# Three of layer 2's eight contraction tiles as sums of fp32r products of halves

## The reference, cut to what matters

```
x = x + x @ W.T + 0.5 * (x @ A[label]) @ Bw.T        # layer 0: one weight, low rank 32
x = x + quantise(x)                                  # layer 1: 8 thresholds, levels 0 to 63
x = x + x @ weight[adapter].T                        # layer 2: a 1024 x 1024 weight per adapter
x = x + (x @ B3[adapter].T) @ A3[adapter].T          # layer 3: low rank 16
```

## Time and profile before

| | us |
|---|---|
| median of 3 runs (464.15 to 465.04) | 464.24 |
| the profiled execution | 464.56 |
| its span, first to last instruction | 462.7 |
| PE busy | 454.7 (98%) |
| VectorE busy | 415.4 (90%) |
| ScalarE busy | 326.7 (71%) |
| a 1 MB load of layer 2's weights, issue to landing (median of 31) | 4.9 |
| a 256 KB store of the output (median of 32) | 2.2 |

### The profile page before, as it was taken

The page is one execution under the profiler, slowest core; times in us unless marked ns, Lnnn a source line. Parts: engine busy times, 40 slices in busy tenths (PEclk is TensorE's granted clock), DMA queues, the critical chain, the costliest instruction groups (busy, mean ns, idle before and its releaser), DMA issues.

```text
span 462.7 us, 7306 instructions
## 1 busy us (share of the span) xinstructions
PE 454.7 (98%) x3006; PEld 410.9 (89%) x3006; DVE 415.4 (90%) x395; ACT 326.7 (71%) x274; POOL 8.1 (2%) x18
## 2 busy tenths in 40 slices
PE   7999999999999999999999999999999999999995
PEld 7899999889998899889998899989998899988884
DVE  4889999999699996999699996999869999999983
ACT  5699979958398747967398754996349848665730
POOL 1000000000000000000000000100000000000000
PEclk9999999999999999999999999999999999999999
DMA  7983430557128534367227543183322522245242
GB/s 279 343 334 104 91 103 1 91 188 279 69 92 221 196 142 159 69 204 279 76 91 188 197 174 126 48 261 132 120 92 91 181 92 96 75 173 180 94 159 91
DMA packets 17941, 69.15 MB, mean 149 GB/s; under 512 B 2421, under 2 KB 3445, under 8 KB 13045
## 3 DMA queue, kind: packets, MB, share of 16 engines
q1 hardware_dynamic: 17044, 62.41, 37.5%
q0 software_dynamic: 864, 6.29, 7.3%
HBM read 54.01 MB, written 8.39 MB: 135 GB/s over the span
## 4 chain that ended last, share of the span: by engine, by line
PE 90%; DMA 3%; issue 2%; DVE 2%; SPq 2%; ACT 1%; DVEq 0%; ACTq 0%
PE l_ps L838 39%; PE l_ps L773 37%; PE l_ps L853 6%; PE bx_ps L872 2%; PE l_ps L783 2%; DMA w_sb<-w 2%; PE bx_ps L799 2%; DMA adapter_ids<-adapters 1%; PE l_ps L902 1%; PE bx_ps L806 1%; PE bx_ps L879 1%; DVE quant L628 1%; ACT cand L439 0%; ACT magnitude L429 0%; SPq L287 0%
## 5 line engine op out<-in xcount | busy, mean ns | idle before, releaser
L838 PE MATMUL l_ps<-x,w_sb 128*128 128x256 f32 x896 | 196.9, 380 | 0.4 <-DVE x L595 0.4
L838 PEld LDWEIGHTS l_ps<-x,w_sb 128*128 128x128 f32 x896 | 169.2, 190 | 25.3 <-issue 2.8
L634 DVE COPY_PREDICATED quant<-mask,cand 128x2048 f32<-128x2048 int8 (+2 forms) x77 | 145.6, 1891 | 0.4
L439 ACT ACTIVATE cand<-x,inv_delta 128x2048 f32<-128x2048 f32 (+2 forms) x88 | 134.5, 1528 | 8.8 <-DVE quant L628 7.0
L449 ACT ACTIVATE mask<-magnitude,thr_bias 128x2048 fp8e5<-128x2048 f32 (+2 forms) x77 | 117.7, 1529 | 13.4 <-DVE quant L634 12.7
L608 DVE TENSOR_SCALAR cand<-cand,delta 128x2048 f32<-128x2048 f32 (+2 forms) x88 | 87.9, 999 | 10.1 <-ACT cand L439 9.8
L616 DVE TENSOR_SCALAR cand<-cand,lower,upper 128x2048 f32<-128x2048 f32 (+2 forms) x88 | 93.4, 1062 | 0.4
L773 PE MATMUL l_ps<-x_hi,w_hi 128*128 128x256 f32 x512 | 87.1, 292 | 0.9 <-DVE x_lo L565 0.9
L773 PE MATMUL l_ps<-x_hi,w_lo 128*128 128x256 f32 x512 | 82.8, 283 | 0.0
L773 PE MATMUL l_ps<-x_lo,w_hi 128*128 128x256 f32 x512 | 82.5, 283 | 0.0
L773 PEld LDWEIGHTS l_ps<-x_hi,w_hi 128*128 128x128 f32 x512 | 71.4, 191 | 6.6 <-issue 4.2
(11 more groups left out here) (66 smaller groups left out, 231.0 us busy)
## 6 DMA issues: line engine op xcount, KB each, us to landing
w_sb<-w SPq DMA_DIRECT2D x31, 1024.0 KB, 4.9
out<-x SPq DMA_DIRECT2D x32, 256.0 KB, 2.2
x_raw<-x SPq DMA_DIRECT2D x15, 512.0 KB, 6.4
x_lo<-x_raw POOLq DMA_DIRECT2D x6, 1024.0 KB, 8.2
a_raw<-a SPq DMA_DIRECT2D x8, 512.0 KB, 3.6
w_sb<-w SPq DMA_DIRECT2D x7, 512.0 KB, 7.4
b_sb<-b SPq DMA_DIRECT2D x8, 256.0 KB, 2.7
a_raw<-a SPq DMA_DIRECT2D x8, 128.0 KB, 6.3
```

The costliest lines, as they stand in the source:

```text
L439: act.activation(cand[:, c % CANDS, 0:n], x2_unit(u), ACT.Identity, bias=ROUND, scale=inv_delta[:, k:k + 1]).then_inc(rounded, 1)
L634: dve.copy_predicated(y, mask[:, m % MASKS, 0:n].bitcast(I8), t).then_inc(merged, 1)
L838: last = nc.tensor.matmul(l2_bank(b, q)[:, i * S:(i + 1) * S], w2_tile(b, o)[:, k * P:(k + 1) * P], x2[:, b % SLOTS, k * S:(k + 1) * S], s ...
```

## The change

For batches 0 to 6 the contraction tiles k = 0, 1, 2 of layer 2 (`EDGE = 3`, the "edges") are no longer multiplied in fp32. Both x2's columns for them (768) and the weights' columns for them (384 of each block) are split into halves, and three fp32r products are summed. The five other tiles stay fp32 and come first in each block. Batch 7 stays fp32 throughout.

- Weights are loaded as eight tiles of 640 columns a batch into a ring of four, and the edges apart, two blocks to a load (384 KB), into a ring of two such pairs.
- ScalarE rounds a pair (`split_edges`) and writes its negation; GpSimd issues a DMA that adds the raw edges to that. Pairs 0 and 1 of a batch stand in that batch's own unit, after groups 5 and 6; pairs 2 and 3 in the next unit, after tests 3 and 4 (for batch 6 in the first part of the last batch, groups 5 and 7).
- VectorE rounds x2's columns and subtracts (`split_x2`) after each unit.
- To make room, layer 0's weights are staged in the candidate buffers, A3 is loaded into the second half of x3 after its store, and batch 7's edges and half of its weights lie in `x_raw`, `cand` and `quant`. `low_parts` and `bx_parts` share a buffer, and B3's padding is loaded for batch 7 alone.
- SyncE's order changes with the loads; the stores of a batch stand behind the last edge load.

```diff
+EDGE = 3
+SPLIT = B - 1
+EW = EDGE * P
+EX = EDGE * S
+RING = 4
+RAW = 4
+HALVES = 4
...
         def w0_stage(n):
-            return w2_sb[:, n // 2 % CHUNKS, n % 2, :]
+            return cand[:, (n // 2 + 1) % CANDS, n % 2 * T * P:(n % 2 + 1) * T * P]
...
+            def load_edges(b, q, adapter):
+                n = 4 * b + q
+                if n >= 2:
+                    sp.wait_ge(w2_added[(n - 2) % 4], 16 * ((n - 2) // 4 + 1))
+                sp.dma_start(two_of(w2_edge, q), w2[bass.ds(adapter, 1), 2 * q:2 * q + 2, :, 0:EW]
+                             .rearrange("l o p w -> p (l o) w")).then_inc(w2_edge_loaded[q], 16)
...
+            for q in range(2, 4):
+                load_edges(0, q, adapter)
+            for s in range(1, B):
+                for o in range(RING, T):
+                    load_w2(s - 1, o, adapter)
+                adapter = adapter_of(s)
+                if s < B - 1:
+                    load_w2(s, 0, adapter)
+                    load_edges(s, 0, adapter)
+                    if s + 3 < B:
+                        load_batch(s + 3)
+                    load_w2(s, 1, adapter)
+                    load_w2(s, 2, adapter)
+                    load_edges(s, 1, adapter)
+                    load_w2(s, 3, adapter)
+                    for q in range(2, 4):
+                        load_edges(s, q, adapter)
...
+                load_b3(s, adapter)
+                for q in range(4):
                     store(s - 1, q)
+                if s < B - 1:
+                    load_a3(s, adapter)
...
+            def add_edges(b, q):
+                pool.wait_ge(w2_neg_done, 4 * b + q + 1)
+                pool.dma_start(two_of(w2_lo, q), two_of(w2_edge, q), accum_op=ALU.add).then_inc(w2_added[q], 16)
...
+            def split_edges(b, q):
+                n = 4 * b + q
+                act.wait_ge(w2_edge_loaded[q], (b + 1) * 16)
+                if n >= 2:
+                    act.wait_ge(l2_done, 2 * (n - 1))
+                act.activation(two_of(w2_hi, q), two_of(w2_edge, q), ACT.Copy).then_inc(w2_hi_done, 1)
+                act.wait_ge(w2_hi_done, n + 1)
+                act.activation(two_of(w2_lo, q), two_of(w2_hi, q).bitcast(F32), ACT.Copy, scale=-1.0)\
+                   .then_inc(w2_neg_done, 1)
...
                     test(u, j)
+                    if j in (3, 4) and 0 < UNITS[u][0] < B - 1:
+                        split_edges(UNITS[u][0] - 1, j - 1)
                     if j + 1 < G:
                         candidate(u, j + 1)
...
+            def split_x2(b):
+                if b > 0:
+                    dve.wait_ge(l2_done, T * b)
+                dve.wait_ge(x2_done, x2_count(b))
+                dve.tensor_copy(x2_hi[:, :], x2[:, b % SLOTS, 0:EX]).then_inc(x2_hi_done, 1)
+                dve.wait_ge(x2_hi_done, b + 1)
+                dve.tensor_tensor(x2_lo[:, :], x2[:, b % SLOTS, 0:EX], x2_hi[:, :].bitcast(F32),
+                                  ALU.subtract).then_inc(x2_split_done, 1)
...
                 if 0 < UNITS[u][0] < B - 1:
                     for q in range(4):
                         finish(UNITS[u][0] - 1, q)
+                if UNITS[u][0] < SPLIT and u > 0:
+                    split_x2(UNITS[u][0])
...
                 for i in range(2):
                     o = 2 * q + i
-                    for k in range(T):
-                        last = nc.tensor.matmul(l2_bank(b, q)[:, i * S:(i + 1) * S], w2_tile(b, o)[:, k * P:(k + 1) * P],
-                                                x2[:, b % SLOTS, k * S:(k + 1) * S], start=(k == 0), stop=(k == T - 1))
-                last.then_inc(l2_done, 1)
+                    pe.wait_ge(w2_loaded[o], (b + 1) * 16)
+                    for k in range(EDGE, T):
+                        last = nc.tensor.matmul(l2_bank(b, q)[:, i * S:(i + 1) * S], w2_block(b, o, k),
+                                                x2[:, b % SLOTS, k * S:(k + 1) * S], start=(i == 0 and k == EDGE),
+                                                stop=False)
+                    last.then_inc(w2_used, 1)
+                if q == 0:
+                    pe.wait_ge(x2_split_done, b + 1)
+                pe.wait_ge(w2_added[q], 16 * (b + 1))
+                for i in range(2):
+                    hi = two_of(w2_hi, q)[:, i, :]
+                    lo = two_of(w2_lo, q)[:, i, :]
+                    for w, v in ((hi, x2_hi), (hi, x2_lo), (lo, x2_hi)):
+                        for k in range(EDGE):
+                            last = nc.tensor.matmul(l2_bank(b, q)[:, i * S:(i + 1) * S], w[:, k * P:(k + 1) * P],
+                                                    v[:, k * S:(k + 1) * S], start=False,
+                                                    stop=(i == 1 and w is lo and k == EDGE - 1))
+                    last.then_inc(l2_done, 1)
```

More of the change, by code:

```diff
@@ L64, in build @@
         w0_lo = sb("w0_lo", [P, T, T * P], F32R)
-        w2_sb = sb("w2_sb", [P, CHUNKS, 2, T * P], F32)
+        w2_sb = sb("w2_sb", [P, RING, T * P - EW], F32)
+        w2_edge = sb("w2_edge", [P, RAW, EW], F32)
+        w2_hi = sb("w2_hi", [P, HALVES, EW], F32R)
+        w2_lo = sb("w2_lo", [P, HALVES, EW], F32R)
+        x2_hi = sb("x2_hi", [P, EX], F32R)
+        x2_lo = sb("x2_lo", [P, EX], F32R)
         x_raw = sb("x_raw", [P, BW], F32)
@@ L115, in build @@
         a0_loaded = sem("a0_loaded")
-        w2_loaded = [sem(f"w2_loaded{q}") for q in range(4)]
+        w2_loaded = [sem(f"w2_loaded{o}") for o in range(T)]
+        w2_edge_loaded = [sem(f"w2_edge_loaded{q}") for q in range(4)]
+        last_w2_loaded = [sem(f"last_w2_loaded{o}") for o in range(T)]
+        w2_used = sem("w2_used")
+        w2_hi_done = sem("w2_hi_done")
+        w2_neg_done = sem("w2_neg_done")
+        w2_added = [sem(f"w2_added{q}") for q in range(4)]
+        x2_hi_done = sem("x2_hi_done")
+        x2_split_done = sem("x2_split_done")
         b3_loaded = sem("b3_loaded")
@@ L340, in add_x @@
                 pool.dma_start(x_lo[:, b % 2, :], x_raw[:, :], accum_op=ALU.add).then_inc(x_added, 16)
-            for b in range(ADDED, B):
-                add_x(b)
+            def add_edges(b, q):
+                pool.wait_ge(w2_neg_done, 4 * b + q + 1)
+                pool.dma_start(two_of(w2_lo, q), two_of(w2_edge, q), accum_op=ALU.add).then_inc(w2_added[q], 16)
+            add_x(2)
+            for q in range(2):
+                add_edges(0, q)
+            for s in range(1, B):
+                if s + 2 < B:
+                    add_x(s + 2)
+                for q in range(2, 4):
+                    add_edges(s - 1, q)
+                if s < SPLIT:
+                    for q in range(2):
+                        add_edges(s, q)
         @block.scalar
@@ L484, in between @@
                         low_rank_hi(s + 2)
+                    if j == 5 and s < SPLIT:
+                        split_edges(s, 0)
                     if j == 6:
                         drain_l0(s + 1, 0)
+                        if s < SPLIT:
+                            split_edges(s, 1)
                     if j == 7:
@@ L805, in sum_low @@
                 pe.wait_ge(low_parts_done, b + 1)
-                nc.tensor.matmul(bx_ps[:, S:2 * S], low_sum[:, :], low_parts[:, :], start=True, stop=True)\
+                nc.tensor.matmul(bx_ps[:, S:2 * S], low_sum[:, :], parts[:, :], start=True, stop=True)\
                   .then_inc(low_sum_done, 1)
@@ L857, in last_layer2 @@
                     if part == len(PARTS) - 2:
-                        last.then_inc(l2_done, 1)
+                        last.then_inc(l2_done, 2)
             def low_rank3(b, q):
@@ L871, in low_rank3 @@
                     rows = slice(k % n * w, (k % n + 1) * w)
-                    last = nc.tensor.matmul(bx_ps[rows, 0:S], b3_sb[:, k, 0:w], x3[:, k * S:(k + 1) * S],
+                    last = nc.tensor.matmul(bx_ps[rows, 0:S], b3_tile(b, k, w), x3[:, k * S:(k + 1) * S],
                                             start=(k < n), stop=(k >= T - n))
@@ L878, in sum_bx @@
                 pe.wait_ge(bx_parts_done, b + 1)
-                nc.tensor.matmul(bx_ps[:, S:2 * S], bx_sum[:, :], bx_parts[:, :], start=True, stop=True)\
+                nc.tensor.matmul(bx_ps[:, S:2 * S], bx_sum[:, :], parts[:, :], start=True, stop=True)\
                   .then_inc(bx_sum_done, 1)
```

195 lines of the change are left out of this document (118 added, 77 removed).

## The result

The changed kernel takes 493.89 us (median of 4 runs, 490.56 to 497.76) against 464.35 beside it (4 runs, 464.15 to 465.04): a ratio of 1.0638 [1.0579, 1.0697]. The forecast was 459.0, the range ended at 464.5. The profiled execution took 494.22, its span is 492.4.

A forecast was written before the change was run, and what follows sets the result against it. PE bounds until batch 6's layer 0 closes, with VectorE close behind afterwards. PE gains 8.6 us, gives back 1.5 and 1.2 in waits, the tail costs 0.7: 464.24 - 5.2 = 459.0 us, range 455.5 to 464.5.

The forecast's parts named there:

- What PE saves: Layer 2 on PE, batches 0 to 6: 1.73 us less a batch, so a step of 50.98 us.
- VectorE's split: VectorE's copy and subtraction of 768 columns of x2 per batch: 0.62 and 0.96 us, together 1.58.
- its wait at bx_split: VectorE's wait for PE's sum of bx through ScalarE: under 1 us where it was 3.5.
- x: Time from a pair's end to the landing of its 384 KB addition: 4.7 us taken, bounds 3.1 and 8.2.
- wait by the prediction's working: PE's wait for quarter 2: 1.5 us in batch 0, 1.2 in 4, 2.0 in 5, 1.4 in 6; else none.
- Quarter 3 has about as much: Quarter 3's addition in batches 1 to 3: about the 1.5 us to spare that quarter 2's has, so no wait.
- the upper bound of 8.2: Longest x for a 384 KB addition, if nothing of the 1024 KB addition's 8.2 us scales with size.
- the rival built on a held issue: VectorE's scale and clip hold GpSimd's issue of quarter 2's additions, up to 2.6 us: 470.1 us, chance 0.15.
- what I cost at nothing: Weight rings, SyncE's stores and A matrix load, layer 0's staging: no cost, at worst each delays a unit by its lateness.
- PE waits for no load after the start: Loads into PE's buffers: none makes PE wait after the start, so no gain was seen in them.
- the total fits: ScalarE's four pairs add 6.8 us a batch to 38.5: 45.3 of a 50.98 us step.
- Rival 2: VectorE becomes the bound with steps of 52.1 us, four of them losing 1.1 more: 461 to 463.4 us, chance 0.16.

The follow-up runs named there:

- the kernel of 463.35: Changed kernel with x's load moved back, quarter 2's edge products behind quarter 3's fp32 blocks, SyncE's loads reordered, pairs of batches 0 and 6 earlier: 463.35 us.
- the first experiment: Changed kernel with the third product using high halves in place of low ones, so PE doesn't wait for the additions, which still run: 463.97 us.
- the kernel of 472.97: Changed kernel with x's load moved back, quarter 2's edge products deferred, pairs of batches 0 and 6 earlier, last batch's free weights issued some 20 us earlier: 472.97 us.

## Why the prediction was wrong

By the page's busy line PE's span of 462.7 is 454.7 of work and 8.0 idle. In the kernel of 463.35 the changed work takes 444.0 at a clock of 1.00. So the 29.7 us between the spans are -10.7 of work, +12.0 because part of it ran at the lower clock (456.0 - 444.0), and +28.4 idle, 27.2 of them for additions. The forecast had the first (-12.1), 6.1 of the last, and nothing of the second. By the first experiment the waits for additions, with the clock behind them, cost 29.9 us (493.89 - 463.97), where the forecast had 3.6 (459.0 against 455.4 without such waits). And without them the kernel takes 463.97, not 455.4: a smaller second miss.

- **What PE saves** was right: 50.96 a step without waits, 50.98 predicted. So were VectorE's split (0.56 and 0.96) and its wait at bx_split (0.46 without PE's waits, "under 1").
- **x** was the first failure: "x = 4.7, the value I take". Alone the addition needs 3.9, with the 0.35 ahead of it 4.3, so scaling by size wasn't the mistake; taking one x for all places was. For quarter 2, with the x measured from the pair's end to the landing, the prediction's own sums give each wait:

| batch | x | wait by the prediction's working | measured |
|---|---|---|---|
| 0 | 6.2 | 1.5 + 1.5 = 3.0 | 2.82 |
| 2 | 6.5 | 1.8 - 1.5 = 0.3 | 0.23 |
| 4 | 6.6 | 1.2 + 1.9 = 3.1 | 3.01 |
| 5 | 6.1 | 2.0 + 1.4 = 3.4 | 3.34 |
| 6 | 8.7 | 1.4 + 4.0 = 5.4 | 5.89 |

- **"Quarter 3 has about as much"** was the second and larger one. There x is 9.3, 9.5, 10.4 and 11.5 in batches 0 to 3, past the upper bound of 8.2. That bound came from 1 MB additions with little traffic beside them (8.2, and 6.9 alone); the rival built on a held issue (470.1) had the right sign, but SyncE's load of x was the main cause: quarter 2's issue was held in batches 0 and 4 alone (1.44 and 1.25 instead of 0.86), and quarter 3's in batches 1 to 3 by 0.8 of the 5 to 7 us that it took beyond 3.9.
- **SyncE's queue**, the cause of that, stood under "what I cost at nothing". There the rule "PE waits for no load after the start" failed too, by 3.15 us before the last batch's weights. I asked whether the loads come in time, not what they do to the addition that is issued beside them, though the code ties them to it: the landing of one addition sets free the loads ahead of the next.
- **The clock** was in no term. PE never stood for long inside a step before (0.40 us at most); with waits of 3 us it did.
- **The slack of ScalarE and VectorE** was the second miss: "the total fits", which holds in the middle steps but not in the first one or at the end. Without any wait for additions and with the two late places mended the time is 462.02. There 10.3 us of work are saved (454.7 - 444.4) and 6.7 come back as idle time (14.7 against 8.0): PE waits 6.1 for ScalarE at three places, and 0.8 more than before for VectorE's drain. ScalarE stands for VectorE ahead of some of them, and which of the two is late first wasn't tried.
- **Rival 2**, VectorE as the bound at 461 to 463.4, has 462.02 in its range by luck. It wanted four steps 1.1 us too long, and they are 50.96, with VectorE at 50.0 in three of them as predicted and 0.44 to 0.50 idle at bx_split. A smaller edge, which gives all three engines less to do, got more out of it: 461.44 against 463.35. The rest of the way to 458.66 is ScalarE's two steps moved up in the last batch; with three tiles PE waits for the same step (1.73 in the kernel of 463.35), so part of that gain may be open there too.

What stays open is what made x of quarter 2 as long as 6.1 to 8.7 where PE waits for it, since no run changed that by itself. In batches 0 to 4 the 1 MB addition of a later x is still under way on GpSimd's own queue when quarter 2's is issued: in batch 4 it was issued 7.3 us earlier, its last transfer ended at 323.75, and quarter 2's first began at 323.67, 2.1 us after its issue. In batch 6 the last batch's loads moved 1.9 MB beside the addition; in the kernel of 472.97, where they went out earlier, 0.5 MB ran beside it, and it landed 4.5 us after the issue instead of 8.3.

## What to carry to other kernels

A transfer on the path is costed in its place, not by its size: list what the same event, or one within a few microseconds, sets free on other queues, and put those bytes ahead of it. A wait of PE can cost its length and then the matmuls behind it at the lower clock, here 12 us on 27. Where a change moves work from the bounding engine to two that have 1 to 6 us of slack in 51, the smaller dose can be the faster one (461.44 against 463.35 here). And a number that falls into a rival's range doesn't show the rival: look for its steps.

## What the runs showed of the hardware that I had not expected

An accumulating DMA of 384 KB needs 3.9 us from issue to landing and one of 1 MB 6.9; of sixteen beside or without work of VectorE and ScalarE one took 1.1 longer, the one whose issue a tensor_scalar held. Of the 28 issues in the changed kernel seventeen took 0.86 to 0.98 us; eleven took 1.25 to 1.95 and ended about 0.1 us after a tensor_scalar of VectorE that they had met. 1 MB on SyncE's queue just ahead of it makes the smaller one 8.1. A subtraction of 128x768 on GpSimd lengthens a tensor_scalar of VectorE that meets it from 1.27 to 2.83.
